# One block's loads moved ahead in the DMA queue, and the operand splits moved to earlier slots, in a convolution and FP8 feed-forward kernel

## The reference, cut to what matters

```python
# cond: per channel h (32 of them), a causal convolution along L = 512 with a generated kernel K
K = 2.0 * einsum('hn,hnl->hl', Ct, exp(P)).real          # (32, 512)
y = irfft(rfft(u, 1024) * rfft(K, 1024))[..., :512] + u * D[:, None]
y = y * (arange(512)[None, :] < length[:, None])[:, None, :]
# ffn on y (128, 32, 512), I = 1376; each input is rounded to FP8 (e4m3) ahead of its product
hidden = silu(linear_fp8(y, gate_w)) * linear_fp8(y, up_w)
x = x + linear_fp8(hidden, down_w)
```

## Time and profile before

| | |
|---|---|
| device time, 3 runs | 324.92, 326.47, 326.5 us; median 326.47 |
| the profiled execution | 325.3 us, of which the span is 323.2 |
| PE busy | 300.3 us, 93% of the span |
| DVE, ACT busy | 213.7 us (66%), 184.0 us (57%) |
| TensorE's granted clock, mean | 0.998 of full |
| chain that ended last | PE 84%, DVE 8%, issue 3%, DMA 2% |
| issue to landing, medians | xt 5.0, toep 8.0 (1024 KB each), out<-in_x 5.4 us |

### The profile page before, as it was taken

The page is one execution under the profiler, slowest core; times in us unless marked ns, Lnnn a source line. Parts: engine busy times, 40 slices in busy tenths (PEclk is TensorE's granted clock), DMA queues, the critical chain, the costliest instruction groups (busy, mean ns, idle before and its releaser), DMA issues.

```text
span 323.2 us, 4639 instructions
## 1 busy us (share of the span) xinstructions
PE 300.3 (93%) x1643; PEld 168.9 (52%) x1671; DVE 213.7 (66%) x436; ACT 184.0 (57%) x250; POOL 13.9 (4%) x25
## 2 busy tenths in 40 slices
PE   2998995999899998999999998999989999999994
PEld 1457752655456554555456553655546554544442
DVE  6979778784946756576746757486756747443433
ACT  4846565565655475564854664663855646544640
POOL 3031000000001000010001000010000000100010
PEclk9999999999999999999999999999999999999999
DMA  6769999400703725073611627055000760070037
GB/s 209 180 182 220 266 281 360 179 1 2 260 2 58 201 52 211 0 129 133 207 52 16 141 103 259 0 91 170 1 3 0 130 260 2 0 132 0 0 58 204
DMA packets 14014, 38.42 MB, mean 119 GB/s; under 512 B 1470, under 2 KB 6558, under 8 KB 11052
## 3 DMA queue, kind: packets, MB, share of 16 engines
q1 hardware_dynamic: 8412, 26.61, 23.5%
q0 software_dynamic: 5584, 11.57, 20.5%
HBM read 33.93 MB, written 15.81 MB: 154 GB/s over the span
## 4 chain that ended last, share of the span: by engine, by line
PE 84%; DVE 8%; issue 3%; DMA 2%; ACT 1%; DVEq 0%; ACTq 0%; SPq 0%
PE gate_ps L636 21%; PE up_ps L636 21%; PE down_ps L574 17%; PE y_ps L560 14%; PE y_ps L541 3%; PE y_ps L556 2%; DVE xl L904 2%; PE y_ps L590 2%; PE down_ps L677 1%; PE down_ps L590 1%; PE y_ps L677 1%; DVE tl L910 1%; DVE hv L942 1%; DMA toep<-kpad_scratch 1%; DMA prm<-in_params 1%
## 5 line engine op out<-in xcount | busy, mean ns | idle before, releaser
L942 DVE SCALAR_TENSOR_TENSOR hv<-sil,fac,up_ps 128x512 f32<-128x512 f32 (+1 forms) x88 | 65.6, 745 | 93.5 <-PE up_ps L636 61.2
L426 ACT ACTIVATE sil<-gate_ps,fac 128x512 f32<-128x512 f32 (+1 forms) x88 | 60.4, 686 | 107.8 <-PE gate_ps L636 104.5
L636 PE MATMUL up_ps<-yq,wu 128*128 128x512 bf16 (+3 forms) x362 | 88.8, 363 | 0.5
L636 PE MATMUL gate_ps<-yq,wg 128*128 128x512 bf16 (+3 forms) x367 | 88.6, 363 | 0.7 <-DVE hv L942 0.5
L574 PE MATMUL down_ps<-wd,hq 128*128 128x512 bf16 (+1 forms) x254 | 66.3, 380 | 0.6
L636 PEld LDWEIGHTS up_ps<-yq,wu 128*128 128x128 bf16 x372 | 36.3, 100 | 38.3
L636 PEld LDWEIGHTS gate_ps<-yq,wg 128*128 128x128 bf16 x372 | 35.9, 100 | 38.8 <-issue 1.2
L560 PE MATMUL y_ps<-xh,th 128*128 128x512 f32 (+2 forms) x84 | 39.9, 475 | 8.9 <-DVE tl L910 4.5
L407 ACT ACTIVATE hq<-hv 128x1024 uint16<-128x1024 uint16 (+1 forms) x48 | 46.8, 976 | 0.0
L398 ACT ACTIVATE yq<-yv 128x1024 uint16<-128x1024 uint16 x32 | 33.6, 1050 | 7.1 <-DVE yv L920 6.5
L574 PEld LDWEIGHTS down_ps<-wd,hq 128*128 128x128 bf16 (+1 forms) x264 | 23.0, 98 | 25.0 <-issue 6.0
(11 more groups left out here) (162 smaller groups left out, 223.0 us busy)
## 6 DMA issues: line engine op xcount, KB each, us to landing
xt<-in_xT SPq DMA_DIRECT2D x8, 1024.0 KB, 5.0
out<-in_x SPq DMA_DIRECT2D x7, 1024.0 KB, 5.4
out<-res POOLq DMA_DIRECT2D x7, 1024.0 KB, 7.8
toep<-kpad_scratch SPq DMA_DIRECT2D x6, 1024.0 KB, 8.0
toep<-kpad_scratch SPq DMA_DIRECT2D x8, 256.0 KB, 4.4
wd<-in_down POOLq DMA_DIRECT2D x1, 1280.0 KB, 22.9
xt<-in_x SPq DMA_DIRECT2D x1, 1024.0 KB, 7.3
out<-xt SPq DMA_DIRECT2D x3, 256.0 KB, 3.8
```

The source lines that it names most:

```text
L426: nc.scalar.activation(sil[b][0:w, :], gate_ps[b][0:w, :], ACT.Silu, scale=fac[0:w, S_GATE:S_GATE + 1]).then_inc(silu_done, 1)
L636: mm = nc.tensor.matmul(ps[b][0:w, cols], wt[:, k, c * P:c * P + w], yq[par][:, version, k, cols], start=(k == 0), stop=(k == LB - 1))
L942: v.scalar_tensor_tensor(hv[c // 2 % 3][0:w, c % 2], sil[b][0:w, :], fac[0:w, S_UP:S_UP + 1], up_ps[b][0:w, :], ALU.mult, ALU.mult).then_i ...
```

## The change

The rows and x of block 2 are loaded right behind block 0's convolutions (rows first), ahead of the third store of K; the wait for that store stands ahead of block 3's loads. The copy of x of block 0 goes behind block 3's loads. Splits start in slots 2 and 7 (3 and 7 in block 0) instead of 4 and 8. In block 0, convolutions that stood in slots 2 and 3 move up by one slot.

```diff
+            sp.wait_ge(y_ready, HB)
+            load_toep(2, 0)
+            load_x_t(2, 0)
             store_k(2)
-
-            sp.wait_ge(y_ready, HB)
-            load_x_t(2, 0)
             sp.wait_ge(k_stored[2], 16)
-            load_toep(2, 0)
-            copy_x(0, 0)
             for g in range(NBLK - 2):
                 if g + 3 < NBLK:
                     sp.wait_ge(y_ready, HB * (g + 2))
                     load_x_t(g + 3, (g + 3) % 2)
                     load_toep(g + 3, (g + 3) % 2)
-                if g:
+                if g == 0:
+                    copy_x(0, 0)
+                else:
                     sp.wait_ge(added[(g - 1) % 2], 16 * ((g - 1) // 2 + 1))
                 copy_x(g + 1, (g + 1) % 2)
...
             def slots(g, par, half, first, ahead):          # ACT; DVE alike with low_x, low_taps
+                splits = FIRST_SPLITS if first else SPLITS
...
-                    if ahead == 2 and c in HIGH_PLAN:
-                        high_x(g + 2, par, half + 1, HIGH_PLAN[c])
-                    if ahead == 2 and c - 1 in HIGH_PLAN:
-                        high_taps(g + 2, par, half + 1, HIGH_PLAN[c - 1])
+                    if ahead == 2 and c in splits:
+                        high_x(g + 2, par, half + 1, splits[c])
+                    if ahead == 2 and c - 1 in splits:
+                        high_taps(g + 2, par, half + 1, splits[c - 1])
...
-                for step, h, distances in CONV_PLAN.get(c, ()):
-                    if step <= ahead and (down or (step, h) != (1, 1)):
+                for step, h, distances in (CONV_PLAN if down else FIRST_CONV_PLAN).get(c, ()):
+                    if step <= ahead:
...
+FIRST_CONV_PLAN = {**CONV_PLAN, 0: [], 1: [(1, 2, [0, 1, 3])], 2: [(1, 2, [2])], 3: [(1, 3, [0])]}
...
-HIGH_PLAN = {4: 0, 8: 1}
+SPLITS, FIRST_SPLITS = {2: 0, 7: 1}, {3: 0, 7: 1}
```

More of the change, by code:

```diff
@@ L982, in slots @@
                         finish_y(g + 1, 1 - par, FINISH_PLAN[c])
[L983 to L986, removed]
+                    if ahead == 2 and c - 1 in splits:
+                        low_x(g + 2, splits[c - 1])
+                    if ahead == 2 and c - 2 in splits:
+                        low_taps(g + 2, splits[c - 2])
                     if c == CH - 1 and ahead == 2:
```

## The result

| | before | after |
|---|---|---|
| median | 326.49 us (4 runs, 324.92 to 327.59) | 315.32 us (4 runs, 315.10 to 315.61) |
| profiled execution, span | 325.3, 323.2 us | 315.1, 313.0 us |
| PE busy | 93% | 96% |

The ratio is 0.9662, with a 95% interval of 0.9621 to 0.9703. The medians lie 11.2 us apart and the two profiled executions 10.2. The forecast was 9.8 us off the profiled execution (315.5) and 316.2 in all, with a range of its own of 314.6 to 317.5, which reaches to 319.8 with the rivals.

What follows compares the result with a forecast made beforehand. PE, busy for 93% of the span, bounds the kernel, so only its waits can be won: 6.74 + 3.1 = 9.8 us, giving 315.5 from the profiled execution, 316.7 from the median; 316.2 taken, range 314.6 to 317.5, to 319.8 with rivals.

Steps and rivals of the forecast that it cites:

- Blocks 1 to 5: Splits two slots earlier end PE's slot 7 waits for `tl`: 6.74 us gained, bounds 0 and 6.74.
- rival 4: Another wait steps in in blocks 1 to 5, giving back half of 6.74 us: 319.5 us; chance 6%.
- Block 0: Second convolution product of slot 7 comes at 51.2 instead of 54.30 us: 3.1 us gained, bounds 0.5 and 4.1.
- The 86 packet pairs per us: Assumed pace of SP's and the weights' queues alternating in block 0; block 2's 512 row packets then need 6.0 us.
- In block 0 the data is late as well: Block 0's `tl` is late also because block 2's rows, issued at 39.12, hold ACT 1.28 us until 48.81.
- The weights (1): Block 0's weights land at 47.5, PE stands 3 us ahead of slot 5, total gain 7.8: 318.1 us; chance 12%.
- x on ACT (2): x lands at 44.6, 3 us too late for ACT; block 0 gains about 0.5: 318.7 us; chance 8%.
- the starved queue (3): SP's queue starved, x so late that ACT and PE's slot 6 stop and the kernel gets slower; chance 3%.
- The stalls labelled "issue" (5): Those of blocks 0 and 5 aren't waits for `tl` and stay; only 5.5 us come: 320.4 us; chance 3%.
- Convolutions one slot up: In block 0 they cover PE's 0.51 us wait for `hv` at slot 2: 0.4 us earlier, bounds 0 and 0.5.
- At nothing: Third store, copies of x and down weights cost 0 us, down weights expected by 57; bounds 0 and 1 us.

Runs made afterwards that it cites:

- experiment 1: Kernel after with only the splits of blocks 1 to 5 moved; SP's order, block 0's splits and convolutions as before: 319.77 us, ratio 0.9784.
- experiment 10: Kernel after with pair 0's splits in slot 3 in all blocks, one slot earlier than before instead of two: 315.39 us, ratio 0.9655.
- experiment 2: Kernel after with only SP's new order kept; all splits in slots 4 and 8, block 0's convolutions as before: 326.42 us, ratio 0.998.
- experiment 3: Kernel after with SP's old order of loads, stores and copy; all splits and convolutions stay moved: 318.87 us, ratio 0.9747.
- experiment 4: Kernel after with the copy of x of block 0 back ahead of block 3's loads: 315.56 us, ratio 0.9653.
- experiment 6: Kernel after with x of block 2 loaded ahead of its rows: 315.34 us, ratio 0.9657.
- experiment 9: Kernel before with 14 useless products of 512 columns in PE's slot 7 of block 0, where it waits for `tl`: 324.54 us, ratio 0.9927.

## Why the prediction was right, and where it was not

- **Blocks 1 to 5** (6.74 us): right. 6.9 us between the two traces and 6.8 in experiment 1. No other wait stepped in (rival 4), and by experiment 10 half of the move would have done.
- **Block 0** (3.1 us): right in size, 3.3 between the traces, of which 0.3 was there before block 0's waits. Most of its steps held: `tl` ended at 49.63 + 0.95 = 50.6 (50.8 forecast), the second product came at 50.99 (51.2), x landed at the latest moment of the 39 to 42 us given, and the weights held PE for 0.42 us (1 us), after landing at 44.6 (45.5). That x landed where it should is partly luck, as two terms were off by about as much. The 86 packet pairs per us were too many: 78 were moved from 31.5 us on, and in the two us before SP's queue had moved only 53 packets per us. By the queue's bytes x was through near 40 us instead of 38.9. It then landed about 2 us behind that, and not the 3.2 that I had taken over from the weights.
- **The reason given for block 0's stall was wrong in one part.** "In block 0 the data is late as well" is true as a row, but the late rows did not cause the stall (experiment 2). I took ACT's wait of 1.28 us for a link of the chain, and did not look whether DVE had had free time; it had none from 47.57 on the earlier trace rows. The load is needed for another reason: a split moved one slot ahead asks for it earlier (experiment 3). The sum did not suffer, since it was worked out from DVE's order.
- **Rivals.** The weights (1) were late by a seventh of what that rival needed. x on ACT (2) cost nothing in the kernel after, yet 1.4 us with the split one slot earlier. For the starved queue (3) there is no sign. The stalls labelled "issue" (5) in blocks 0 and 5 were waits for `tl`: they went with it.
- **Convolutions one slot up** (0.4 us, taken up by the other waits): at most some tenths, not settled. **At nothing**: right for the copies and the down weights (experiment 4), with 1.8 us to spare there even in the old order.
- **From the profiled execution to the median** is the step that missed something. I subtracted 9.8 from both 325.3 and 326.47 and took a value between, without asking why the two differ. (The low end of the forecast's own range is 325.3 - 10.84 = 314.5 by its sum, not 314.6.) The mean granted clock of each execution goes with the difference. Of the 33 executions of the kernel before in the three sets, one has 0.998 and took 325.1 us; 19 have 0.992 to 0.995, with a median of 326.4; 13 have 0.989 or 0.990, with a median of 327.6. The profiled one had 0.998. The four executions of the kernel after have 0.999 or 1.0. A difference of 0.003 alone says nothing: in experiment 6 executions at 0.997 and at 1.0 lie within 0.5 us. So the profiled execution was one of the few without a loss of clock, and most executions of before lost 1.3 us or more. Of the 11.2 us at the median, 10.2 lie between two executions at full clock, and I put the rest down to clock that the 3.4 us stall had cost. That split is inferred from the mean clocks, as the one trace of before is of an execution without the loss. Experiment 1 shows where the loss falls: its slot 8 takes 58.23 - 54.30 = 3.93 us, and that of the kernel after 53.95 - 51.46 = 2.49, 1.4 us less; the products just ahead of slot 8 lose the rest of the 1.7. Experiment 9 shows that the stall is the cause, as the loss goes when PE works through it. Timeline of PE, kernel after:

```profile
51.46 1.04 PE L637 MATMUL gate_ps<-yq,wg 128*128 128x512 bf16 x4
...
53.95 1.03 PE L637 MATMUL gate_ps<-yq,wg 128*128 128x512 bf16 x4
```

The Trainium skill, page "TensorE: Matmul & The Clock Gate", section "HAM oscillation — how this bites in real kernels", says that a matmul engine left waiting for data comes back at half its clock. The trace of experiment 1 agrees (0.60 behind a stall of 3.44 us), and that of experiment 9, with 0.42 us left of the stall, stays at 1.00. The profiled execution of before does not agree: it stood for 3.44 us as well and came back at 1.00.

What stays open is where the 13 slowest executions of before lost their further 1.2 us, as none of them has a trace here, and why the clock fell behind the same stall in most executions but not in all.

## What to carry to other kernels

Read the cost of a stall from the distance of starts against a slot without one, and before naming its cause check that the engine which ends it was itself waiting; here it was full, so only the order of its work or an earlier place for it could help. A transfer moved forward pays only together with the work that asks for it earlier, and moving that work too far turns a late transfer into a wait for the whole in-order engine (1.4 us here for one slot). If the profiled execution lies apart from the median, compare the granted clocks of the executions first: a stall of PE can cost more than its own length (here 1.7 us on top of 3.4).

## What the runs showed of the hardware that I had not expected

- Behind one stall of 3.4 us the granted clock fell to half for part of the next 4 us (0.60 over 54 to 58 us in experiment 1, 0.57 in experiment 2), and behind one of 3.3 us as well (0.50 over 52 to 54 us in experiment 3). By the mean clocks it fell in 32 of the 33 executions of before, but not in the profiled one. The five stalls of 1.0 to 1.1 us in blocks 1 to 5 of before, one to a block, left it at 1.00. Views by windows, experiment 2 and before:

```profile
54.00:58.00 4.00, 4.00 (x13) 0.57 1.03 414
```

```profile
66.00:260.00 194.00, 187.51 (x944) 1.00 0.34 94
```

- Fourteen useless products of 512 columns in that stall took 2.8 us off the median, 2.4 by the ratio (experiment 9).
- With two queues at work the weights landed about 3 us behind the point where their 2.29 MB had been moved in the kernel before (37.3 and 40.4 us) and 2.5 us in the kernel after (42.2 and 44.6), and x about 2 us. These are estimates from the bytes of the queues by windows. 1 MB of x took 15.2 us from issue to landing behind other rows, against a median of 4.9.
